# Mamba block with a state scan on one core: each accumulation one slot later, and result stores later in the DMA queue's order

## The reference, cut to what matters

```python
xz = x @ W_in;  x_branch, z = split(xz)               # 512 -> 2 x 1024
xc = silu(depthwise_conv(x_branch, 4 taps) + conv_b)  # causal
ssm = xc @ W_x;  B, C = 16 values each per token;  dt = softplus(ssm[-1] + dt_bias)
h = h * exp(dt * A) + (dt * xc) * B                    # per channel, 16 states, over the tokens
y = sum over the 16 states of h * C
out = ((y + xc * D_param) * silu(z)) @ W_out
```

## Time and profile before

| | |
|---|---|
| time, median of 3 runs | 5925.71 us (5920.22 to 5927.35) |
| profiled execution, its own time | 5929.52 us |
| its span, first to last instruction | 5926.9 us |
| TensorE busy | 4948.3 us, 83% |
| VectorE busy | 5042.1 us, 85% |
| ScalarE busy | 2804.8 us, 47% |
| GpSimd busy | 3615.0 us, 61% |
| mean granted TensorE clock | 0.951 |

### The profile page before, as it was taken

One profiled execution on the slowest core, in us unless ns is written; L12 is line 12 of the kernel. 1 busy time (PEld: TensorE's weight loads), 2 busy tenths in 40 slices (PEclk: granted clock), 3 DMA queues, 4 the chain that ended last, 5 costly groups with the idle time before them and its releaser, 6 DMA issues.

```text
span 5926.9 us, 78012 instructions
## 1 busy us (share of the span) xinstructions
PE 4948.3 (83%) x21764; PEld 3214.7 (54%) x21764; DVE 5042.1 (85%) x6343; ACT 2804.8 (47%) x4579; POOL 3615.0 (61%) x2810
## 2 busy tenths in 40 slices
PE   1799999999997888788787888878878787887867
PEld 1688888888883444444444444444444444444444
DVE  7666666676661999999999989989999998999998
ACT  1111111111112675665666657566565665656654
POOL 4333333333320886787877778777777877868785
PEclk9999999999998899999999999999999999999978
DMA  2111111111112112122121221212222221222111
GB/s 73 32 43 42 42 41 41 42 42 42 41 38 99 63 56 79 59 86 70 57 74 65 78 74 61 71 60 77 75 66 65 68 78 62 77 67 69 62 58 50
DMA packets 211700, 362.55 MB, mean 61 GB/s; under 512 B 26208, under 2 KB 58976, under 8 KB 207216
## 3 DMA queue, kind: packets, MB, share of 16 engines
q1 hardware_dynamic: 211312, 358.17, 19.2%
HBM read 287.80 MB, written 70.29 MB: 60 GB/s over the span
## 4 chain that ended last, share of the span: by engine, by line
DVE 24%; PE 18%; issue 15%; ACT 5%; POOL 5%; DVEq 1%; DMA 0%; SPq 0%; ACTq 0%; POOLq 0%
DVE hs L1094 15%; DVE acc L1108 8%; PE ht L1211 7%; POOL v L918 4%; PE mm L1160 4%; PE mm L1200 3%; PE mm L1151 2%; ACT decay L1055 1%; PE mm L1175 1%; PE mm L1168 1%; DVEq L793 1%; ACT xc L980 1%; DVE rtb L1080 1%; ACT L1055 1%; ACT L980 1%
## 5 line engine op out<-in xcount | busy, mean ns | idle before, releaser
L918 POOL TENSOR_TENSOR v<-u,b_rep 128x512 f32<-128x512 f32 x2048 | 2564.8, 1276 | 833.8 <-DVE hs L1094 445.2
L1211 PEld LDWEIGHTS ht<-ident,hs 128*128 128x128 f32 x8192 | 1016.6, 148 | 1683.9 <-issue 1136.2
L1055 ACT ACTIVATE decay<-dt,a_neg 128x512 f32<-128x512 f32 x2048 | 1393.8, 687 | 948.9 <-DVE hs L1094 941.0
L1211 PE MATMUL ht<-ident,hs 128*128 128x128 f32 x8192 | 1349.8, 291 | 554.9 <-DVE hs L1094 396.4
L1108 DVE SCALAR_TENSOR_TENSOR acc<-ht,c_now,acc 128x512 f32<-128x512 f32 x2048 | 1493.5, 729 | 160.3 <-PE ht L1211 158.1
L1094 DVE TENSOR_TENSOR_SCAN hs<-decay,v 128x512 f32<-128x512 f32 x1024 | 1244.2, 1215 | 115.4 <-POOL v L918 112.2
L1094 DVE TENSOR_TENSOR_SCAN hs<-decay,carry,v 128x512 f32<-128x512 f32 x1024 | 1305.4, 1275 | 3.4 <-ACT decay L1055 3.4
L489 ACT ACTIVATE sg<-gate 128x512 f32<-128x512 f32 (+1 forms) x192 | 108.2, 563 | 1331.6 <-PE up L535 1331.6
L1160 PE MATMUL mm<-xb,tap_diag 128*128 128x512 f32 (+3 forms) x1024 | 543.6, 637 | 109.7 <-issue 108.2
L1200 PE MATMUL mm<-w_out,yt 128*128 128x512 f32 x1024 | 546.3, 634 | 43.4 <-ACT xb L965 30.4
L1151 PE MATMUL mm<-x_in,w_in 128*128 128x512 f32 x1024 | 531.9, 626 | 28.4 <-DMA x_in<-xnt_d 17.1
(11 more groups left out here) (124 smaller groups left out, 6936.7 us busy)
## 6 DMA issues: line engine op xcount, KB each, us to landing
b_rep<-ssm_d SPq DMA_DIRECT2D x512, 256.0 KB, 3.8
tap_diag<-tap_d SPq DMA_DIRECT2D x128, 256.0 KB, 3.7
rtb<-res_d SPq DMA_DIRECT2D x128, 256.0 KB, 3.4
xt<-in_L_attn_x SPq DMA_DIRECT2D x64, 256.0 KB, 2.8
xnt_d<-xntb SPq DMA_DIRECT2D x64, 256.0 KB, 2.7
rt<-in_L_attn_x SPq DMA_DIRECT2D x64, 256.0 KB, 2.6
res_d<-rt SPq DMA_DIRECT2D x64, 256.0 KB, 2.0
x_in<-xnt_d SPq DMA_DIRECT2D x16, 1024.0 KB, 4.8
```

Source lines behind the costliest of these rows:

```text
L918: nc.gpsimd.tensor_tensor(v[k % 2][:, j, :], u[g][:, j, :], b_rep[k % 4][:, :], ALU.mult).then_inc(v_ready, 1)
L1055: nc.scalar.activation(decay[n % 4][:, :], dt[g][:, j, :], ACT.Exp, scale=a_neg[:, GD * g + j, s:s + 1]).then_inc(decay_ready, 1)
L1211: last = nc.tensor.transpose(ht[n % 2][:, j, :], h[k % 2][:, j, t * P:(t + 1) * P], ident[:, :])
```

## The change

Accumulations move from four slots behind the scan to five: `add_state(n - 5)` stands after `scan(n)`, and the copy of `c_now` stands at slot 4 in place of 3. TensorE's order stays as it is: it transposes block `n - 4` at slot `n`. In the queue's list the eight stores and the loads tied to them stand later, and so does `ssm`; the taps, `x_in` and `x_z` keep their steps.

```diff
+    LAG = 5
-    SP_AT = {2: [("load", 1, 0), ("load", 1, 1)], 5: [("tap", 2), ("store", 1, 0)],
-             6: [("store", 1, 1), ("load", 1, 2), ("load", 1, 3)], 7: [("tap", 3)],
-             9: [("store", 1, 2)], 10: [("tap", 4)], 11: [("tap", 5), ("store", 1, 3)], 16: [("tap", 6)],
-             17: [("tap", 7), ("x_in",)], 19: [("tap", 0)], 20: [("load", 0, 0), ("load", 0, 1)], 21: [("tap", 1)],
-             22: [("ssm",)], 23: [("store", 0, 0)], 25: [("store", 0, 1), ("load", 0, 2), ("load", 0, 3)],
-             27: [("store", 0, 2)], 28: [("store", 0, 3)], 31: [("x_z",)]}
+    SP_AT = {2: [("load", 1, 0), ("load", 1, 1)], 5: [("tap", 2)], 7: [("tap", 3)], 8: [("store", 1, 0)],
+             9: [("store", 1, 1), ("load", 1, 2)], 10: [("tap", 4), ("load", 1, 3)], 11: [("tap", 5)], 13: [("store", 1, 2)],
+             15: [("store", 1, 3)], 16: [("tap", 6)], 17: [("tap", 7), ("x_in",)], 19: [("tap", 0)],
+             20: [("load", 0, 0), ("load", 0, 1)], 21: [("tap", 1)], 23: [("ssm",)], 25: [("store", 0, 0)],
+             26: [("store", 0, 1), ("load", 0, 2)], 27: [("load", 0, 3)], 28: [("store", 0, 2)], 29: [("store", 0, 3)],
+             31: [("x_z",)]}
...
         def part(c):
             for n in range(4 * SLOTS):
-                before, m = (c, n - 4) if n >= 4 else (c.plus(-1), n + 4 * SLOTS - 4)
+                before, m = (c, n - LAG) if n >= LAG else (c.plus(-1), n + 4 * SLOTS - LAG)
                 if c.exists(NC):
                     scan(c, n)
                 if before.exists(NC):
                     add_state(before, m)
-                if n == 3 and c.exists(NC):
+                if n == LAG - 1 and c.exists(NC):
                     wait(dve, summed, c.at(128, 0))
```

## The result

The changed kernel takes 5821.85 us (median of 4 runs, 5820.11 to 5827.07) against 5926.53 us before in the same comparison: a ratio of 0.9827, 95% interval 0.981 to 0.9844. It is faster, by 105 us or 1.7%. The forecast was 5814 us. The profiled execution has a span of 5824.2 us, 102.7 less than before.

The account below looks back on a forecast made before the run. VectorE was taken to set the pace, with only its idle time to win. Terms: -87.2 - 14.6 - 15 + 5 = -112 us, giving a median of 5814 us; range for 8 in 10, 5788 to 5850 us.

Parts of the forecast that it names:

- The long wait: Chunks 1 to 14, first unit of `cv` 3: TensorE waits for `tap` 3, queued behind `store` (1,1) and `load` (1,3).
- a fetch of instructions: Rival, 3%: the 8 us TensorE waits at `cv` 3 are not the tap's but an instruction fetch; time 5916 us.
- -87.2 and -14.6 us for the waits and those behind them: VectorE's fourteen 5.2 to 7.1 us waits for transposes vanish (-87.2 us), and the next accumulation's second wait too (-14.6 us).
- 0 for all other moves in the queue: Stores, their loads and `ssm` issued later than before cost nothing, hidden behind VectorE.
- +5 us for new waits: Later accumulation: a state's block 3 has 1.77 us for its transposes, too little at low clock; bounds 0 and 35 us.
- blocks 1 and 2: Middle blocks of each state: their transposes are released one slot later and due one slot later, so no difference.
- Rival 1: Late results for ScalarE, late decays or late block 3 cost 3 to 5 us in each of 14 chunks; 5855 to 5885 us; 13%.
- -15 us for small waits: After slot 40 TensorE no longer idles at taken banks, so VectorE's small waits and decay waits shrink; bounds 0 and 25.7 us.
- The seams: Between chunks and where the loop turns round: 31.0 us of accumulation waits (39 waits), forecast to gain nothing.
- The rival of the scans waiting for `turned`: Each state's first scan waits 0.2 to 0.5 us for block 3's transposes, clock lower; slower kernel, 5993 us at 0.35 us; 6%.
- The later accumulation is worth about nothing: Accumulating five slots behind instead of four: forecast as -15 us of small waits won and +5 us of new ones.

## Why the prediction was right, step by step

- **The long wait is `tap` 3's, held by a store and a load: right, and shown.** Moved alone it gives the whole 105 us; moved back it takes 39 us again. That "issue" hid a DMA, and not a fetch of instructions, follows from the same two runs.
- **-87.2 and -14.6 us for the waits and those behind them: right.** With the queue's order alone the accumulations' wait falls by 94 us and the time by 103 us (5927.92 to 5824.72), against 101.8. The time falls further than that wait also because the scans' wait for `v` goes from 6.5 us to 1.8, which had been forecast as no gain. That the second wait of each pair goes with the first is seen. That it was the clock which made it was not tried by itself, but the run with `tap` 3 behind the store shows the clock at 0.54 right behind a wait of 0.9 us.
- **0 for all other moves in the queue: right.** Both runs with the old list and only `tap` 3 moved in it tie with their partners.
- **+5 us for new waits: the term that was mis-sized.** They measured 16.8 us more for decays (6.6 to 23.4), 10.9 us for scans behind their transposes (under 10 had been forecast) and 11.8 us more for additions to `rtb`, and 2.2 us less for `v` (6.5 to 4.3): 37 us, or 39 with the idle time that has no named cause. That is above the prediction's own upper bound of 35 us. The step that failed is the one that said that nothing is lost with blocks 1 and 2. It compared the transposes only with the accumulations, while everything that TensorE does between them comes later too. The addition of slot 29 and ScalarE's copy of slot 42 had no slot to spare. The run with both moved shows it: 12.5 us of each kind of wait go. Rival 1 named the copy, at 3 to 5 us a chunk, but held it for unlikely; 2.7 us a chunk came beside the forecast.
- **-15 us for small waits: too small.** The accumulations lost 134.2 - 101.8 = 32 us of them, more than the bound of 25.7 us. As forecast, TensorE no longer finds its banks taken: its waits for `rtb` at line 1186 (now 1187), 56 us, are gone, and those for ScalarE's `xb` fell from 30.4 to 7.4 us. That this is the reason is argued and not tried. The seams, put at 0, cost the accumulations less too, but part of it came back as scans that wait behind them (1.20 us in the case shown).
- **That the sum came out near was in part luck.** The two errors, 17 us and 34 us, go opposite ways and cancel by half: -15 + 5 = -10 was forecast, and -32 + 39 = +7 came out (27.1 before the scans and 11.8 before the additions). With the 101.8 that makes 95 us. The rest of the span's 102.7 was not forecast: 1.9 us of idle time before the accumulations that has no named cause, and the 5.5 us of busy time.
- **The later accumulation is worth about nothing: right as a sum, wrong as a reading.** Between the kernel with the queue's order alone and the changed one it is a gain of 40 us before the accumulations (62.5 to 22.7) and a loss of 42 us before scans and additions. With the old queue the loss wins (+16 us), with the new one they balance (-3 us, within the noise), and with two tasks moved it comes out 13 us ahead in the medians.
- **The rival of the scans waiting for `turned`: its place and its kind were right, its size small at five slots** (10.9 us). It decides at six. The row read for it, the four slow transposes at a seam, doesn't tell transposes from idleness: TensorE had stood idle 2.32 us right before them.

## What to carry to other kernels

In a queue that is kept strictly in order, an entry that waits for a result holds back every load behind it (here one entry was worth the whole 105 us). A store is wanted by nobody for a long time, a load by the next matmul, so read the queue for what stands behind each wait, and move the urgent entry ahead of it first. When one engine's release moves by a slot, don't only compare the pair of instructions that the wait is between: everything in that engine's list moves, and each consumer placed without slack can show up as a wait elsewhere. Test the halves of a change alone, for a gain may sit in one and a loss in the other.

## What the runs showed that I had not expected

- A load of 256 KB is quicker or slower by what was issued just ahead of it. `tap` 3 reached its matmul in 2.8 to 3.5 us when only a store stood ahead of it, and in 4.0 to 5.3 us behind two loads and a row of B, in 14 cases each. Which of the entries ahead makes the difference was not tried.
- One microsecond of waiting in TensorE, with 3 us at a granted clock of 0.54 behind it, cost VectorE 2.6 us. Three quarters of that are waits for late decays and products 14 to 25 us later.
- The step from five slots to six costs what the step from four to five doesn't hint at: +16 to -13 us for the one, depending on the rest of the lists, +705 us (6526.41 - 5821.85) for the other.
